# Softmax row sums in an attention block: one ones-column matmul per four key tiles, after a second vector add

## The chip, the cores and the metric

The kernel runs on all 8 cores of one Trainium2 chip. Every core executes the same program on its own data, and no core waits for another. The metric is the device time of the slowest core, in microseconds (us).

## The reference, cut to what matters

One transformer layer on x of shape (4, 2048, 2048): layer norm, latent attention with 16 heads of 128, residual, layer norm, a gated FFN with fp8 weights, residual.

```python
lat = rmsnorm(x @ wkv_a_w.T, norm_w)
kv = lat @ wkv_b_w.T
q = (x @ wq_w.T + wq_b).reshape(B, S, H, DH)        # B=4, S=2048, H=16, DH=128
scores = jnp.einsum('bqhd,bkhd->bhqk', q, k) * scale
scores = jnp.where(mask, scores, -jnp.inf)          # causal
attn = jax.nn.softmax(scores, axis=-1)
o = jnp.einsum('bhqk,bkhd->bqhd', attn, v).reshape(B, S, H * DH)
x = x + o @ out_w.T + out_b
gate = silu(layernorm(x) @ gate_w8 * gate_scale)    # 2048 -> 6144, fp8 weights
x = x + ((gate * (layernorm(x) @ up_w8 * up_scale)) @ down_w8) * down_scale
```

## The kernel before, in words

Core c takes batch entry c // 2 and one half of its 2048 positions as queries: 1024 queries, held as two blocks `qb` of 512. Keys and values are made for all 2048 positions. The stages follow each other, most of them with a barrier (every engine waits for every semaphore) between them: layer norm and transposes; the latent projection (L331); the query projection (L377); then twice (`hg` 0 and 1, eight heads each) the key projection (L440), a bound on the scores (L457 to L490), the value projection (L500) and attention (L514 to L597); then the normalization by the row sums (L602 to L627), the output projection (L665 to L699), a barrier (L700), a second layer norm (L705 to L724), gate and up (L736 to L782) and down (L789 to L857).

In attention an outer step is one head and one query block, called a block here; `pair_idx` counts the 32 blocks of a core, 16 in each half `hg`. Inside a block the loop at L545 runs over key tiles of 128, called slots: 12 slots for `qb` 0, 16 for `qb` 1. A slot is a score matmul (L551: keys as weights, 512 queries moving) into one of three PSUM banks, an exponential on ScalarE (L559) that writes a bf16 tile of 128x512 into one of eight places `PSL`, and, for the four diagonal slots of each block, a multiplication by a mask on VectorE (L566). In the blocks of `qb` 0 these are slots 0 to 3, in those of `qb` 1 slots 4 to 7. Two slots form a slot pair `p` (6 or 8 in a block). For each pair VectorE adds the two tiles (L577) into `PADD[p % 2]`, and `emit_pair(p)` queues on TensorE a ones-column matmul (L531), which adds the column sums of `PADD` to the row `PS[5]`, and then the two value matmuls (L539), which add to `PS[po]`. A program writes every engine's queue in this order: score 2p, score 2p+1, then `emit_pair(p - 1)`; after the last scores of a block `emit_pair` of its last pair comes alone. A score waits for the exponential three slots back (L550), because of its PSUM bank. The ones-column matmul waits for its `PADD` (L526), and all that stands behind it on TensorE's in-order queue waits with it: the two value matmuls and the next pair's two scores. At a block's end VectorE waits for the last value matmul, copies the row of sums (L588), which a DMA takes to its row of `F32A` (L591), and evicts the output (L594).

All waits on VectorE's work count on one semaphore, `sV`. `kb.wait` (L73) emits a wait only if that engine has not yet waited for this semaphore at that value or a higher one (L77).

In the FFN the weight loads of gate and up are issued from GpSimd (L744, L746) into two buffers; iterations 0 and 1 wait for the last matmul of the output projection, `mm_f[15]` (L741).

Of the kernel before, what the change touches and what calls it, by code (L numbers as in the profile page):

```python
# [10 lines left out]
BF16 = mybir.dt.bfloat16  # L11
# [82 lines left out]
def build_nc():  # L94
# [39 lines left out]
    sb = lambda n, sh, dt: es.enter_context(nc.sbuf_tensor(n, sh, dt))  # L134
# [42 lines left out]
    EPSC = sb("EPSC", [128, 2], F32)  # L177
    SEL = sb("SEL", [32, 384], F32)
    X4 = sb("X4", [128, 2048], BF16)

    PS = [pt(f"PS{i}", [128, 512], F32) for i in range(6)]
    PT = [pt("PT0", [128, 1024], BF16), pt("PT1", [128, 1024], BF16)]

    kb = KB(nc)
# [28 lines left out]
    try:  # L213
# [208 lines left out]
        av_ring = {}  # L422
        av_by = {}
        g_ctr = [0]
        bcast_S = [None]

        for hg in range(2):
# [86 lines left out]
            for i8 in range(8):  # L514
                h = hg * 8 + i8
                for qb in range(2):
# [2 lines left out]
                    npair = nsl // 2  # L519
                    po = 2 + (pair_idx % 2)  # L520
                    gstart = g_ctr[0]
                    rdy = {}
                    padd_by = {}

                    def emit_pair(p, i8=i8, qb=qb, po=po, gstart=gstart, npair=None, nsl=None):
                        kb.wait("tensor", "sV", padd_by[p])  # L526
                        if p == 0 and pair_idx > 0:
                            kb.wait("tensor", "sV", linv_by_pair[pair_idx - 1])
                            if pair_idx > 1:
                                kb.wait("tensor", "sV", otev_by_pair[pair_idx - 2])  # L530
                        kb.op("tensor", lambda e, p=p, isf=(p == 0), isl=(p == npair - 1): e.matmul(  # L531
                            PS[5][0:1, 0:512], ONESCb[:, 0:1], PADD[p % 2],
                            start=isf, stop=isl))
                        for i in (2 * p, 2 * p + 1):
                            kt_i = slot_lists[qb][i]
                            pi_i = (gstart + i) % 8
                            av_by[(pair_idx, i)] = av_ring[gstart + i] = kb.op(
                                "tensor", lambda e, pi_i=pi_i, kt_i=kt_i, i8=i8,
                                isf=(i == 0), isl=(i == nsl - 1), po=po: e.matmul(  # L539
                                    PS[po][:, :],  # L540
                                    BIG0[:, VOFF + kt_i * 1024 + i8 * 128:VOFF + kt_i * 1024 + i8 * 128 + 128],
                                    PSL[pi_i],
                                    start=isf, stop=isl), inc="sT")

                    for j, kt in enumerate(slots):  # L545
# [25 lines left out]
                        if j % 2 == 1:  # L571
                            p = j // 2
                            kb.wait("vector", *rdy[j - 1])
                            kb.wait("vector", *rdy[j])
                            if p >= 2:
                                kb.wait("vector", "sT", av_by[(pair_idx, 2 * (p - 2))])
                            padd_by[p] = kb.op("vector", lambda e, p=p, gstart=gstart: e.tensor_add(  # L577
                                PADD[p % 2], PSL[(gstart + 2 * p) % 8],
                                PSL[(gstart + 2 * p + 1) % 8]), inc="sV")
                            if p >= 1:  # L580
                                emit_pair(p - 1, npair=npair, nsl=nsl)
                    emit_pair(npair - 1, npair=npair, nsl=nsl)
                    g_ctr[0] += nsl
                    pgl = pair_idx % 16
                    kb.wait("vector", "sT", av_by[(pair_idx, nsl - 1)])
# [43 lines left out]
        mm_f = {}  # L629
# [106 lines left out]
        for io in range(48):  # L736
            bufp = io % 2
            if io >= 2:
                kb.wait("gpsimd", "sT", gu_mm[io - 2])
            else:  # L740
                kb.wait("gpsimd", "sT", mm_f[15])  # L741
            gin = A(gatew, io * 128, [[6144, 128], [128 * 6144, 16], [1, 128]])
            uin = A(upw, io * 128, [[6144, 128], [128 * 6144, 16], [1, 128]])
            g1 = kb.dma("gpsimd", lambda e, gin=gin, bufp=bufp: e.dma_start(  # L744
# [196 lines left out]
```

How the kernel before makes its waits and increments, by code:

```python
        def w(e, fn=fn, h=h, n=n):  # L67
            fn(e).then_inc(h, n)
# [4 lines left out]
    def wait(self, eng, name, v):  # L73
        if v is None or v <= 0:
            return
        key = (eng, name)
        if self.lastwait.get(key, 0) >= v:
            return
        self.lastwait[key] = v
        h = self.semh[name]
        self.ops[eng].append(lambda e, h=h, v=v: e.wait_ge(h, v))
```

## Time and profile before

| | us |
|---|---|
| three runs | 2452.5, 2599.4, 2604.5 (median 2599.4) |
| the profiled execution, its own time | 2458.6 |
| its span on the slowest core (core 1) | 2456.8 |
| spans of the eight cores | 2429.6 to 2456.8 |

The span is from the first to the last instruction of a core. The engines' busy times overlap, so they don't add up to it. PE is TensorE's matmuls, PEld its weight loads, DVE VectorE, ACT ScalarE, POOL GpSimd. In a timeline row "x2" are two instructions that follow each other, with the time from the start of the first to the end of the last, and the bracket is how long the engine had been idle and who ended it. The time of a matmul is its latency; back to back they follow each other faster than that.

### The profile page before, as it was taken

The numbers are of one execution on the slowest core, as the hardware profiler recorded it, in microseconds if no ns is written. First come the engines' busy times: TensorE is split into PE (matmuls) and PEld (weight loads), VectorE is DVE, ScalarE is ACT, GpSimd is POOL, SyncE is SP. The second block draws the span as 40 slices with busy tenths as digits, with TensorE's granted clock in tenths as the row PEclk, the third lists the DMA queues.
The fourth block names the chain that finished last, engine by engine and source line by source line (L and its number), as shares of the span: only waits on it lengthen the run. The fifth ranks groups of instructions, "written<-read, shape, count | busy, mean of one in ns | idle before, by whom it ended". The sixth has DMA issues, their size and how long they took to land.

```text
span 2456.8 us, 24409 instructions; the slowest of 8 cores (2429.6 to 2456.8 us)
## 1 busy us (share of the span) xinstructions
PE 1901.9 (77%) x8678; PEld 817.2 (33%) x8678; DVE 467.2 (19%) x1005; ACT 682.6 (28%) x961; POOL 236.8 (10%) x238
## 2 busy tenths in 40 slices
PE   1297944767664767657884699999999997999898
PEld 1243422211122211111442344444444443444443
DVE  3500034144434244422111300000000000000000
ACT  4621200576720766700112412211222121000000
POOL 0001100000000000000110011111111110111110
PEclk9998968899987999955997799999999998999999
DMA  6416712000011000020999378888787876988886
GB/s 149 155 18 60 71 13 28 0 1 1 1 13 22 1 1 1 1 26 0 152 157 162 77 36 40 38 38 40 37 42 35 42 36 40 80 74 77 75 79 65
DMA packets 455047, 121.94 MB, mean 50 GB/s; under 512 B 384977, under 2 KB 450706, under 8 KB 451858
## 3 DMA queue, kind: packets, MB, share of 16 engines
q0 software_dynamic: 382144, 60.90, 42.7%
q1 hardware_dynamic: 72786, 59.48, 8.4%
q8 instruction: 73, 1.20, 0.2%
q14 instruction: 44, 0.36, 0.1%
HBM read 239.83 MB, written 16.78 MB: 104 GB/s over the span
## 4 chain that ended last, share of the span: by engine, by line
PE 65%; DMA 11%; DVE 10%; ACT 7%; issue 6%; DVEq 0%; ACTq 0%; SPq 0%; POOL 0%; POOLq 0%
PE PS L759 13%; PE PS L764 13%; PE PS L818 13%; PE PS L539 3%; PE PS L377 3%; DMA WT<-outwT 3%; PE PS L677 3%; PE PS L440 3%; PE PS L619 3%; PE PS L500 2%; DVE SQB L577 2%; PE PS L331 2%; PE PS L531 2%; DMA WT<-wqT 2%; DMA F32A<-xb 2%
## 5 line engine op out<-in xcount | busy, mean ns | idle before, releaser
L818 PE MATMUL PS<-BIG,W 128*128 128x512 bf16 x1536 | 338.7, 380 | 17.1 <-DMA W<-downw 17.1
L759 PE MATMUL PS<-BIG,W 128*128 128x512 bf16 x1536 | 347.7, 379 | 1.4 <-DMA W<-upw 1.4
L764 PE MATMUL PS<-BIG,W 128*128 128x512 bf16 x1536 | 347.2, 379 | 0.0
L818 PEld LDWEIGHTS PS<-BIG,W 128*128 128x128 fp8e4 x1536 | 150.4, 98 | 193.4 <-issue 20.8
L759 PEld LDWEIGHTS PS<-BIG,W 128*128 128x128 fp8e4 x1536 | 150.3, 98 | 183.3 <-issue 3.1
L764 PEld LDWEIGHTS PS<-BIG,W 128*128 128x128 fp8e4 x1536 | 150.3, 98 | 181.2
L531 PE MATMUL PS<-SQB,ONESCb 128*1 128x512 bf16 x224 | 87.2, 389 | 114.5 <-DVE SQB L577 114.5
L559 ACT ACTIVATE X<-PS,BIASC,SCL 128x512 bf16<-128x512 f32 x224 | 157.0, 774 | 67.7 <-PE PS L551 67.7
L780 DVE TENSOR_TENSOR BIG<-PB 128x512 bf16<-128x512 bf16 x96 | 40.8, 425 | 625.0 <-ACT PB L776 625.0
L551 PE MATMUL PS<-BIG 128*128 128x512 bf16 x448 | 137.4, 389 | 24.6 <-ACT PB L559 12.0
L193 PE MATMUL PT<-IDB,XHB 128*128 128x128 bf16 x384 | 44.8, 310 | 125.4 <-DVE XHB L267 125.4
L773 ACT ACTIVATE PB<-PS,GSCc 128x512 bf16<-128x512 f32 x96 | 66.0, 688 | 269.8 <-PE PS L759 269.8
L677 PE MATMUL PS<-BIG,WT 128*128 128x512 bf16 x512 | 124.2, 399 | 19.8 <-DMA WT<-outwT 19.8
L776 ACT ACTIVATE PB<-PS,USCc 128x512 bf16<-128x512 f32 x96 | 66.0, 687 | 259.0 <-PE PS L764 259.0
L377 PE MATMUL PS<-BIG,WT 128*128 128x512 bf16 x512 | 114.8, 384 | 16.0 <-DMA WT<-wqT 15.8
L827 ACT ACTIVATE F32A<-PS,DSCc 128x512 f32<-128x512 f32 x32 | 22.0, 687 | 377.1 <-PE PS L818 377.1
L744 POOL DMA_DIRECT2D W<-gatew x48 | 54.8, 1143 | 620.5 <-PE PS L764 599.1
L440 PE MATMUL PS<-LATT,WT 128*128 128x512 bf16 x256 | 71.8, 444 | 52.4 <-DVE BIG L448 38.3
L619 PE MATMUL PS<-F32A,SEL 32*128 32x512 f32 x64 | 65.3, 1122 | 43.0 <-DVE SEL L613 43.0
L559 ACT ACTIVATE PB<-PS,BIASC,SCL 128x512 bf16<-128x512 f32 x112 | 81.0, 773 | 60.5 <-PE PS L551 60.5
L852 DVE TENSOR_TENSOR F32A<-PS,F32A 128x512 f32<-128x512 f32 x32 | 22.1, 692 | 378.1 <-PE PS L841 378.1
L687 ACT ACTIVATE F32A<-PS,OUTBc 128x512 f32<-128x512 f32 x32 | 22.0, 687 | 242.2 <-PE PS L677 242.2
(106 smaller groups left out, 1566.5 us busy)
## 6 DMA issues: line engine op xcount, KB each, us to landing
F32A<-xb SPq DMA_DIRECT2D x16, 1024.0 KB, 5.1
W<-gatew POOLq DMA_DIRECT2D x48, 256.0 KB, 8.6
W<-upw POOLq DMA_DIRECT2D x48, 256.0 KB, 10.4
W<-downw POOLq DMA_DIRECT2D x48, 256.0 KB, 9.2
WT<-wqT POOLq DMA_DIRECT2D x16, 512.0 KB, 6.7
F32A<-xb SPq DMA_DIRECT2D x32, 256.0 KB, 5.0
WT<-outwT POOLq DMA_DIRECT2D x16, 512.0 KB, 9.2
res_scr<-F32A SPq DMA_DIRECT2D x32, 256.0 KB, 5.5
```

The lines of the kernel that those rows point to most:

```text
L377: mmct = kb.op("tensor", lambda e, c=c, pi=pi, ot=ot, qb=qb: e.matmul(PS[pi][:, :], WT[:, (ot % 2) * 2048 + c * 128:(ot % 2) * 2048 + (c + ...
L440: mmct = kb.op("tensor", lambda e, c=c, tb=tb, i8=i8: e.matmul(PS[tb][:, :], WT[:, (i8 % 2) * 2048 + c * 128:(i8 % 2) * 2048 + (c + 1) * 128],
L531: kb.op("tensor", lambda e, p=p, isf=(p == 0), isl=(p == npair - 1): e.matmul(PS[5][0:1, 0:512], ONESCb[:, 0:1], PADD[p % 2], start=isf, s ...
L539: isf=(i == 0), isl=(i == nsl - 1), po=po: e.matmul(PS[po][:, :], BIG0[:, VOFF + kt_i * 1024 + i8 * 128:VOFF + kt_i * 1024 + i8 * 128 + 12 ...
L551: t_s = kb.op("tensor", lambda e, sb_=sb_, i8=i8, kt=kt, qb=qb, h=h: e.matmul(sb_[:, :], BIG0[:, KOFF + i8 * 2048 + kt * 128:KOFF + i8 * 2 ...
L559: exp_ring[g] = kb.op("scalar", lambda e, pi=pi, sb_=sb_, qb=qb, kt=kt: e.activation(PSL[pi], sb_[:, :], AFT.Exp, bias=BIASC[:, qb * 16 + ...
L619: mm_by[p] = mmb = kb.op("tensor", lambda e, s=s: e.matmul(PS[2 + s][:, 0:512], SEL[0:32, s * 128:(s + 1) * 128], F32A[0:32, 2560:3072], s ...
L677: mmct = kb.op("tensor", lambda e, c=c, pi=pi, dt=dt, qb=qb: e.matmul(PS[pi][:, :], WT[:, (dt % 2) * 2048 + c * 128:(dt % 2) * 2048 + (c + ...
L759: mmg = kb.op("tensor", lambda e, c=c, qb=qb, bufp=bufp, pb=pb: e.matmul(PS[pb][:, :], W8[:, bufp * 2048 + c * 128:bufp * 2048 + (c + 1) * ...
L764: mmu = kb.op("tensor", lambda e, c=c, qb=qb, bufp=bufp, pb=pb: e.matmul(PS[pb + 1][:, :], W8[:, 4096 + bufp * 2048 + c * 128:4096 + bufp ...
L773: s_g = kb.op("scalar", lambda e, io=io, pb=pb: e.activation(PB[:, 0:512], PS[pb][:, :], AFT.Silu, scale=GSCc[:, io:io + 1]), inc="sS")
L818: isl=(t3 == 2 and cc == 15): e.matmul(PS[pi][:, :], W8[:, slot * 2048 + cc * 128:slot * 2048 + (cc + 1) * 128], fuse_ap(c, qb), start=isf ...
```

## The change

Two edits.

1. In attention the results of two adds are added once more: after each odd pair, VectorE adds `PADD[0]` and `PADD[1]` into a new tile `PADD2`, and one ones-column matmul on `PADD2` takes the place of the two on `PADD`. The old `emit_pair` is split: `emit_lmm(q2)` queues the ones-column matmul for the pairs 2*q2 and 2*q2+1, and `emit_av(p)` the two value matmuls. For even `p` from 2 on, `emit_lmm` of the two pairs before comes right ahead of `emit_av(p - 1)`; at a block's end `emit_lmm` of the last two pairs comes ahead of the last `emit_av`. A new write to `PADD` waits for the last `PADD2` add instead of for a value matmul. `PADD2` is one tile: its next write waits for the ones-column matmul that read it.
2. In the FFN the wait of GpSimd for `mm_f[15]` ahead of the first two weight loads is taken out.

```diff
+    PADD2 = sb("PADD2", [128, 512], BF16)
...
-                    def emit_pair(p, i8=i8, qb=qb, po=po, gstart=gstart, npair=None, nsl=None):
+                    def emit_lmm(q2, nq=nq):
+                        kb.wait("tensor", "sV", padd2_by[q2])
+                        if q2 == 0 and pair_idx > 0:
+                            kb.wait("tensor", "sV", linv_by_pair[pair_idx - 1])
+                        lmm_by[q2] = last_lmm[0] = kb.op(
+                            "tensor", lambda e, isf=(q2 == 0), isl=(q2 == nq - 1): e.matmul(
+                                PS[5][0:1, 0:512], ONESCb[:, 0:1], PADD2[:, 0:512],
+                                start=isf, stop=isl), inc="sT")
+
+                    def emit_av(p, i8=i8, qb=qb, po=po, gstart=gstart, nsl=None):
                         kb.wait("tensor", "sV", padd_by[p])
-                        if p == 0 and pair_idx > 0:
-                            kb.wait("tensor", "sV", linv_by_pair[pair_idx - 1])
-                            if pair_idx > 1:
-                                kb.wait("tensor", "sV", otev_by_pair[pair_idx - 2])
-                        kb.op("tensor", lambda e, p=p, isf=(p == 0), isl=(p == npair - 1): e.matmul(
-                            PS[5][0:1, 0:512], ONESCb[:, 0:1], PADD[p % 2],
-                            start=isf, stop=isl))
+                        if p == 0 and pair_idx > 1:
+                            kb.wait("tensor", "sV", otev_by_pair[pair_idx - 2])
...
                             if p >= 2:
-                                kb.wait("vector", "sT", av_by[(pair_idx, 2 * (p - 2))])
+                                kb.wait("vector", "sV", padd2_by[p // 2 - 1])
+                            elif last_padd2[0]:
+                                kb.wait("vector", "sV", last_padd2[0])
...
+                            if p % 2 == 1:
+                                q2 = p // 2
+                                kb.wait("vector", "sV", padd_by[p])
+                                if q2 >= 1:
+                                    kb.wait("vector", "sT", lmm_by[q2 - 1])
+                                elif last_lmm[0]:
+                                    kb.wait("vector", "sT", last_lmm[0])
+                                padd2_by[q2] = last_padd2[0] = kb.op("vector", lambda e: e.tensor_add(
+                                    PADD2[:, 0:512], PADD[0], PADD[1]), inc="sV")
                             if p >= 1:
-                                emit_pair(p - 1, npair=npair, nsl=nsl)
-                    emit_pair(npair - 1, npair=npair, nsl=nsl)
+                                if p % 2 == 0 and p >= 2:
+                                    emit_lmm((p - 2) // 2)
+                                emit_av(p - 1, nsl=nsl)
+                    emit_lmm((npair - 2) // 2)
+                    emit_av(npair - 1, nsl=nsl)
...
             if io >= 2:
                 kb.wait("gpsimd", "sT", gu_mm[io - 2])
-            else:
-                kb.wait("gpsimd", "sT", mm_f[15])
```

## Rows read from the trace of the kernel before

**Rows 1.** The windows view: both attention halves, the key projection, gate/up. First its columns.

```profile
core 1: us, PE busy (x) PEld busy (x) DVE busy (x) ACT busy (x) POOL busy (x), PEclk, DMA share, GB/s
475.00:695.00 220.00, 153.88 (x554) 43.14 (x554) 91.25 (x205) 155.11 (x223) 7.30 (x15) 0.98 0.00 1
...
702.00:760.00 58.00, 35.98 (x128) 13.65 (x128) 19.47 (x32) 0.00 (x0) 4.46 (x6) 0.86 0.17 16
...
820.00:1048.00 228.00, 159.72 (x555) 43.95 (x555) 91.28 (x205) 159.02 (x226) 7.30 (x15) 0.96 0.00 1
...
1386.00:2054.00 668.00, 664.18 (x3076) 300.61 (x3073) 41.77 (x98) 133.30 (x193) 105.01 (x92) 1.00 0.77 37
```

**Rows 2.** The groups of instructions by line over the whole execution.

```profile
L531 PE MATMUL PS<-SQB,ONESCb 128*1 128x512 bf16 x224 | 87.2, 389 | 114.5 <-DVE SQB L577 114.5
...
L577 DVE TENSOR_TENSOR SQB<-X 128x512 bf16<-128x512 bf16 x112 | 47.6, 425 | 102.2 <-PE PS L551 49.0 <-PE PS L539 29.8 <-ACT X L559 20.4
```

**Rows 3.** The waits of the first attention half, 475 to 695 us.

```profile
PE PS L531 <- DVE SQB L577: 57.3, 73, 1.4
...
ACT X L559 <- PE PS L551: 33.1, 30, 2.0
...
ACT PB L559 <- PE PS L551: 29.7, 27, 2.0
```

**Rows 4.** The timeline inside a block of `qb` 0 (weight loads left out).

```profile
480.10 1.45 ACT L559 ACTIVATE X<-PS,BIASC,SCL 128x512 bf16<-128x512 f32 x2 [0.27 <-PE PS L551]
...
481.72 0.42 DVE L577 TENSOR_TENSOR SQB<-X 128x512 bf16<-128x512 bf16 x1 [1.29 <-PE PS L551]
...
482.29 0.38 PE L531 MATMUL PS<-SQB,ONESCb 128*1 128x512 bf16 x1 [0.37 <-DVE SQB L577]
...
482.60 0.60 PE L539 MATMUL PS<-X,BIG 128*128 128x512 bf16 x2
...
483.04 0.59 PE L551 MATMUL PS<-BIG 128*128 128x512 bf16 x2
...
483.52 1.45 ACT L559 ACTIVATE SQB<-PS,BIASC,SCL 128x512 bf16<-128x512 f32 x2 [0.27 <-PE PS L551]
...
485.14 0.42 DVE L577 TENSOR_TENSOR SQB<-SQB 128x512 bf16<-128x512 bf16 x1 [1.29 <-ACT SQB L559]
```

**Rows 5.** The timeline over a block's end, and the ends of the two blocks behind it.

```profile
486.46 0.81 PE L551 MATMUL PS<-BIG 128*128 128x512 bf16 x3
486.73 0.68 DVE L588 COPY LINV<-PS 1x512 f32<-1x512 f32 x1 [1.17 <-PE PS L539]
486.94 2.79 ACT L559 ACTIVATE X<-PS,BIASC,SCL 128x512 bf16<-128x512 f32 x4 [1.97 <-PE PS L551]
...
502.27 0.68 DVE L588 COPY LINV<-PS 1x512 f32<-1x512 f32 x1 [1.24 <-PE PS L539]
...
514.32 0.68 DVE L588 COPY LINV<-PS 1x512 f32<-1x512 f32 x1 [1.24 <-PE PS L539]
```

**Rows 6.** The timeline: a vector add behind a vector mask that it needs, twice.

```profile
475.21 0.42 DVE L566 TENSOR_TENSOR PB<-PB,MASKS 128x512 bf16<-128x512 bf16 x1 [0.24 <-ACT PB L559]
475.74 0.43 DVE L577 TENSOR_TENSOR SQB<-PB 128x512 bf16<-128x512 bf16 x1
...
491.84 0.43 DVE L566 TENSOR_TENSOR PB<-PB,MASKS 128x512 bf16<-128x512 bf16 x1 [0.24 <-ACT PB L559]
492.44 0.43 DVE L577 TENSOR_TENSOR SQB<-PB 128x512 bf16<-128x512 bf16 x1 [0.17 <-DVE PB L566]
```

**Rows 7.** The same loop at low granted clock: the windows view, then the timeline.

```profile
561.40:564.70 3.30, 3.30 (x9) 0.73 (x9) 0.42 (x1) 2.47 (x4) 0.00 (x0) 0.52 0.00 0
...
561.53 0.59 PE L531 MATMUL PS<-SQB,ONESCb 128*1 128x512 bf16 x1
562.05 1.03 PE L539 MATMUL PS<-X,BIG 128*128 128x512 bf16 x2
562.87 1.06 PE L551 MATMUL PS<-BIG 128*128 128x512 bf16 x2
563.61 1.45 ACT L559 ACTIVATE SQB<-PS,BIASC,SCL 128x512 bf16<-128x512 f32 x2 [0.83 <-PE PS L551]
```

**Rows 8.** The groups of instructions by line: the first weight loads of gate and up.

```profile
L759 PE MATMUL PS<-BIG,W 128*128 128x512 bf16 x1536 | 347.7, 379 | 1.4 <-DMA W<-upw 1.4
```

More of the change, by code:

```diff
@@ L424, in build_nc @@
         g_ctr = [0]
+        last_lmm = [None]
+        last_padd2 = [None]
         bcast_S = [None]
@@ L521, in build_nc @@
                     gstart = g_ctr[0]
+                    nq = npair // 2
                     rdy = {}
                     padd_by = {}
-                    def emit_pair(p, i8=i8, qb=qb, po=po, gstart=gstart, npair=None, nsl=None):
-                        kb.wait("tensor", "sV", padd_by[p])
-                        if p == 0 and pair_idx > 0:
-                            kb.wait("tensor", "sV", linv_by_pair[pair_idx - 1])
-                            if pair_idx > 1:
-                                kb.wait("tensor", "sV", otev_by_pair[pair_idx - 2])
-                        kb.op("tensor", lambda e, p=p, isf=(p == 0), isl=(p == npair - 1): e.matmul(
-                            PS[5][0:1, 0:512], ONESCb[:, 0:1], PADD[p % 2],
-                            start=isf, stop=isl))
+                    padd2_by = {}
+                    lmm_by = {}
+                    def emit_lmm(q2, nq=nq):
[7 more added lines that the diff above has]
+                    def emit_av(p, i8=i8, qb=qb, po=po, gstart=gstart, nsl=None):
+                        kb.wait("tensor", "sV", padd_by[p])
+                        if p == 0 and pair_idx > 1:
+                            kb.wait("tensor", "sV", otev_by_pair[pair_idx - 2])
                         for i in (2 * p, 2 * p + 1):
```

## The prediction

> **What bounds the kernel now.** I read the windows view first, cut at the stages, because a change to attention is worth what that stage lets through. In gate and up TensorE is busy for 664 of 668 us. In the two attention halves it is busy for 154 of 220 and 160 of 228 us, and ScalarE, the next engine, for 155 and 159; nothing is full there [rows 1]. So the stage is a chain of engines waiting for each other. The groups and the waits name its links: TensorE stands for 114.5 us ahead of the ones-column matmul L531, always for the vector add L577 [rows 2], and ScalarE stands for 33.1 and 29.7 us in the first half for scores [rows 3].
>
> The timeline gives the chain link by link [rows 4]. From start to start: vector add 481.72, ones-column matmul 482.29 (+0.57, of which 0.42 is the add), value matmuls 482.60 (+0.31), scores 483.04 (+0.44), exponentials 483.52 (+0.48), the next add on this chain 485.14 (+1.62: two exponentials, 1.45, and 0.17). Sum 3.42 us. That add belongs to the slot pair two further on. Two such chains interleave, one of even and one of odd pairs, so two pairs take 3.42 us: the exponentials that start at 480.10 and at 483.52 are those of one chain, 3.42 apart. ScalarE has 2 x 1.45 = 2.90 of work in it at most and isn't the bound.
>
> Check at the length of a block. From the first score at a block's start: 0.48 to the exponentials, 2.79 for four of them, 0.17 to the add of the odd pair (3.44), then the odd chain turns 2 times (6 pairs) or 3 times (8 pairs), then add to scores 0.57 + 0.31 + 0.44 = 1.32. That makes 11.60 and 15.02 us. Measured between ends of blocks: 514.32 - 502.27 = 12.05 and 502.27 - 486.73 = 15.54 [rows 5]. The rest, about 0.5 in each, I put down to the masks. The odd chain thus sets the length of a block, and the block's last pair is an odd one.
>
> **The change, part by part.**
>
> *Ones-column matmuls removed.* 224 become 112 [rows 2]. Each holds the queue for 0.31 us (start of L531 to start of L539, [rows 4]). But which leave the chain? Even pairs lose theirs: their chain becomes 3.42 - 0.31 = 3.11 us. Odd pairs keep one, since `emit_lmm` stands ahead of `emit_av` of the odd pair, also at the block's end. Had the removed ones been on the path they would be worth 112 x 0.31 = 34.7 us. By the block sum above they lie on the even chain, which has to wait for the odd one in TensorE's order, so I count nothing. What hides them is the odd chain; without that cover they are worth the 34.7.
>
> *Vector adds inserted.* 3 for each of 16 blocks and 4 for each of 16: 112. Each stands behind the odd pair's add and waits for its result; the ones-column matmul waits for it, and behind that on TensorE the odd pair's value matmuls and the next two scores, and so the next exponentials. Its duration isn't in the trace; the nearest rows are L577, same shape and type, 0.425 us [rows 2]. The wait of a vector instruction for the one before it: mask end 475.63 to add 475.74 is 0.11, mask end 492.27 to add 492.44 is 0.17 [rows 6]. So an insertion costs 0.53 to 0.60 us, and the odd chain becomes 3.95 to 4.02 us. All 112 stand on it: 59 to 67 us. I take the middle, 63.
>
> The Trainium skill has another price: VectorE: DVE Perf Modes, section on the TRN2 errata, gives (58 + elements / speed-up) cycles at 0.96 GHz for SBUF to SBUF. With 512 elements at 2x that is an estimate of 0.33 us where this trace has 0.425. By it the adds would cost 0.10 us less each, 11 us in all. The measured row decides.
>
> *Other new waits.* The write to `PADD` now waits for the last `PADD2` add on VectorE's own queue; that lies a pair back. `PADD2` waits for the ones-column matmul that read it, two pairs back. Both are over before the exponentials are in: nothing, and if the second wasn't, it would come to a part of one 0.38 us matmul. The old wait for a value matmul two pairs back goes; in the steady rows the add starts 0.17 us after the exponentials' end in any case [rows 4], so it gives nothing. VectorE itself has room: 91 of 220 us plus 56 x 0.425 = 24.
>
> *The clock.* In the halves the granted clock is 0.98 and 0.96 [rows 1], that is 2.4 GHz with short stretches at 1.2. A stretch at half clock lowers the mean by half its share, so 2 x 0.02 x 220 + 2 x 0.04 x 228 = 27 us are low. In one, TensorE had stood for the masks after a block's end, and then the links were 0.52, 0.82 and 0.74 instead of 0.31, 0.44 and 0.48 [rows 7]: 0.85 us more for a turn of the chain. Now TensorE has 554 matmuls in the first half's 220 us (2.5 per us); after the change it has 56 fewer in some 31 us more (2.0 per us). The stage nearest to that is the key projection, 128 matmuls of this width in 58 us (2.2 per us), and its granted clock is 0.86: 28% of the time low [rows 1]. The same share of 448 + 63 us is 143 us, 116 more than now. A low turn takes 4.0 + 0.85, so each low us costs 0.85 / 4.85 = 0.175 us: 20 us. Bounds: 0 if the pauses stay as they are, and 90 if every turn is low (112 x 0.85 = 95, less the 27 x 0.175 = 5 already paid). I take 20, from the nearest row.
>
> *The FFN wait.* The barrier at L700 has made GpSimd wait for TensorE's semaphore at a value that `mm_f[15]` is part of, and `kb.wait` drops a wait already covered. So no instruction goes: 0 us. If one did, the only stall on these loads is 1.4 us [rows 8].
>
> **Sum.** 2458.6 (the profiled execution's own time; its span is 1.8 less) + 63 + 20 = 2541.6, say 2542 us, +3.4%. This stands on the level of the lowest of the three runs (2452.5); the median, 2599.4, lies 5.7% above that execution, and no trace here shows such a run.
>
> **The rivals.**
>
> 1. *The add is hidden and the matmul pays* (opposite side). If VectorE were done before TensorE gets to the ones-column matmul, 34.7 us would go: 2424. For it speaks only that VectorE is 41% busy. Against it: TensorE waits there for the add 73 times in the first half, 57.3 us, 0.78 each [rows 3]. It decides once the sum add ends before TensorE reaches the matmul, some 0.8 + 0.5 us earlier than these rows make it. Chance 0.04.
>
> 2. *The chains share.* If even and odd chains evened out through ScalarE's and TensorE's order, each two pairs would cost the mean of the two changes: (0.56 - 0.31) / 2 = 0.125 us, 112 of them 14 us: 2473, within 2%. For it: both go through the same queues. Against it: the even chain cannot start its scores before the odd one's value matmuls, and the block's end is the odd one. Chance 0.10, with what lies between it and the forecast.
>
> 3. *The clock falls for good.* 67 + 90 us: 2616. The mechanism is a longer pause of TensorE in every turn (the 0.53 to 0.60 of the add) with fewer matmuls between. Against it: at the low clock the same loop kept TensorE busy through the whole stretch [rows 7], and the clock then came back. The Trainium skill speaks for it: TensorE: Matmul & The Clock Gate, section HAM oscillation, says that pauses between bursts send the array back to half rate each time anew. Chance 0.07, again with what lies above my range.
>
> 4. *The FFN edit starts the loads sooner*: at most 1.4 us, changes no chance.
>
> **How the numbers follow.** The forecast has 0.79. Its own range runs from 59 + 0 less a margin for the sharing (2510) to 67 + about twice the clock's price (2566). Rivals 1 and 2 hold 0.14 and rival 3 0.07; none of the three can be left out whole without the others passing 2 in 10, so the range is the forecast's, a few us wider at both ends for what lies between the cases: 2505 to 2572 should hold 0.8. This kernel's measurement can tell about 2%, 49 us, from no change. Below -2% there is nearly nothing, since even all of 34.7 isn't 49: 0.02. Within: the rest of rivals 1 and 2, 0.12 (a cheaper add alone, 0.42 with no wait behind it, would still be 47 us). Slower: the forecast and rival 3, 0.86.
>
> **What would show it.** In the changed kernel's timeline inside a block: an add of `PADD2` 0.53 to 0.60 us behind the odd pair's add; the ones-column matmul 0.57 behind that; odd adds 3.95 to 4.02 apart, where now it is 3.42; value matmuls of even pairs 0.57 behind their add. Ends of blocks 12.05 + 1.7 and 15.54 + 2.2 us apart. In the windows view attention halves some 40 us longer, with a granted clock near 0.86; the FFN unchanged. I am wrong if the add to `PADD2` ends before TensorE has finished the work queued ahead of its matmul, if it takes much less than 0.42 us, or if the clock stays as it is (then 2522) or stays low (then 2616).

## The result and the profile after

| | before | after |
|---|---|---|
| median of the runs, us | 2458.0 (10 runs) | 2537.7 (9 runs) |
| ratio to before, 95% interval | | 1.0325, 1.0302 to 1.0348 |
| span of the profiled execution, slowest core | 2456.8 | 2533.1 |
| first to last sum copy of each attention half, both added up | 423.1 | 502.1 |

The change makes the kernel 3.25% slower, some 80 us, and attention holds all of it. (Single executions of any of these kernels are some per cent longer, with one die at a lower clock; the ratios leave them out, and two of the three times shown ahead of the prediction were such.)

The last row of the table is read from the copies of the sums that end the blocks, 15 blocks in each half. The page of the changed kernel, engine row:

```profile
PE 1901.2 (75%) x8410; PEld 822.8 (32%) x8566; DVE 517.3 (20%) x1117; ACT 687.0 (27%) x961; POOL 237.2 (9%) x238
```

PEld 8566 is 112 less than before and DVE 1117 is 112 more: the matmuls that went, the adds that came. (The count of PE itself lacks some records in this trace; before, loads and matmuls were 8678 each.) POOL is x238 in both kernels. The wait that the FFN edit takes out isn't counted there, but `kb.wait` never emitted it, since the barrier at L700 had covered its value: the edit changes nothing in the program.

The windows view of the changed kernel: both attention halves, then the 668 us of gate and up. It answers to [rows 1] and has its columns: stretch, length, busy time of PE, PEld, DVE, ACT and POOL with the number of instructions, granted clock, DMA share, GB/s.

```profile
475.00:736.00 261.00, 160.62 (x489) 46.34 (x498) 114.65 (x258) 156.60 (x220) 7.34 (x15) 0.85 0.00 1
861.00:1129.00 268.00, 163.15 (x494) 46.91 (x504) 116.55 (x262) 161.23 (x227) 7.34 (x15) 0.84 0.00 1
1449.00:2117.00 668.00, 654.14 (x3002) 300.11 (x3064) 49.16 (x111) 138.86 (x199) 105.14 (x92) 0.99 0.78 38
```

The halves, 220 and 228 us before, are 261 and 268 long; ScalarE does nearly the same work in them, 157 and 161 us (155 and 159 before); the granted clock went from 0.98 and 0.96 to 0.85 and 0.84. Gate and up is as it was: 665.4 us from its first to its last matmul, 665.5 before (its PE count lacks records too).

The groups by line answer to [rows 2]:

```profile
L536 PE MATMUL PS<-PADD,ONESCb 128*1 128x512 bf16 x112 | 48.7, 435 | 148.2 <-DVE PADD L599 148.2
...
L599 DVE TENSOR_TENSOR PADD<-SQB 128x512 bf16<-128x512 bf16 x112 | 47.6, 425 | 17.2 <-DVE SQB L589 13.1 <-PE PS L561 0.7
```

Half as many ones-column matmuls (L536), but TensorE stands longer ahead of them: 148.2 us, 1.32 for each, where 224 had 114.5. All of it ends with the new add, L599. It takes 425 ns, as the first add does.

One turn of the odd chain in the timeline of the changed kernel, at full clock; it answers to [rows 4], and one row from the next turn is added:

```profile
513.62 0.43 DVE L589 TENSOR_TENSOR SQB<-SQB 128x512 bf16<-128x512 bf16 x1 [2.38 <-ACT SQB L569]
...
514.22 0.42 DVE L599 TENSOR_TENSOR PADD<-SQB 128x512 bf16<-128x512 bf16 x1 [0.17 <-DVE SQB L589]
514.78 0.38 PE L536 MATMUL PS<-PADD,ONESCb 128*1 128x512 bf16 x1 [0.79 <-DVE PADD L599]
515.09 0.61 PE L549 MATMUL PS<-SQB,BIG 128*128 128x512 bf16 x2
...
515.54 0.59 PE L561 MATMUL PS<-BIG 128*128 128x512 bf16 x2
...
516.01 1.45 ACT L569 ACTIVATE X<-PS,BIASC,SCL 128x512 bf16<-128x512 f32 x2 [0.79 <-PE PS L561]
517.56 0.43 DVE L589 TENSOR_TENSOR SQB<-X 128x512 bf16<-128x512 bf16 x1 [1.75 <-ACT X L569]
...
518.74 0.38 PE L536 MATMUL PS<-PADD,ONESCb 128*1 128x512 bf16 x1 [2.17 <-DVE PADD L599]
```

From start to start: first add to second +0.60, to the ones-column matmul +0.56, value matmuls +0.31, scores +0.45, exponentials +0.47, next add +1.55. Sum 3.94, where it was 3.42. The second add costs 0.60; the last link is 0.07 shorter than before (1.55 for 1.62). In the next turn TensorE stands for 2.17 us ahead of the ones-column matmul.

The ends of four blocks on core 1 of the changed kernel answer to [rows 5]:

```profile
552.90 0.68 DVE L612 COPY LINV<-PS 1x512 f32<-1x512 f32 x1 [1.24 <-PE PS L549]
570.50 0.68 DVE L612 COPY LINV<-PS 1x512 f32<-1x512 f32 x1 [1.24 <-PE PS L549]
...
637.35 0.68 DVE L612 COPY LINV<-PS 1x512 f32<-1x512 f32 x1 [1.24 <-PE PS L549]
651.00 0.68 DVE L612 COPY LINV<-PS 1x512 f32<-1x512 f32 x1 [1.24 <-PE PS L549]
```

A long block takes 17.60 and a short one 13.65. These are, to 0.01 us, the shortest of their kinds, and nearly all others are longer by a stretch at the low clock. Before, the shortest were 12.05 and 15.47, and most blocks took just that (the 15.54 of [rows 5] is the first whole block of a half).

The two can now be told apart. 30 blocks (16 long and 14 short) at their shortest are 416.2 us before and 472.4 after: 56.2 us, or 0.53 for each second add. Measured as a mean of the eight cores they are 422.3 and 501.9. What lies over the shortest, 6.1 and 29.5 us, is 23.4 more. Nearly all of it lies in blocks that hold a stretch at the low clock (all but 1.0 us before and 0.1 after), so I put it down to the clock.

### The profile page after: what moved, and what is told of

Read it like the earlier page. It is cut to its first block, busy times and chain, and to the rows that moved or that the text cites. A ratio compares the mean times of both kernels' runs of the same rounds, so it can differ in the third digit from the quotient of the medians.

```text
span 2533.1 us, 24253 instructions; the slowest of 8 cores (2504.6 to 2533.1 us)
## 1 busy us (share of the span) xinstructions
PE 1901.2 (75%) x8410; PEld 822.8 (32%) x8566; DVE 517.3 (20%) x1117; ACT 687.0 (27%) x961; POOL 237.2 (9%) x238
## 4 chain that ended last, share of the span: by engine, by line
PE 63%; DVE 11%; DMA 11%; ACT 7%; issue 7%; DVEq 1%; ACTq 0%; SPq 0%; POOL 0%; POOLq 0%
PE PS L781 13%; PE PS L786 13%; PE PS L840 13%; PE PS L549 4%; PE PS L378 3%; PE PS L701 3%; DMA WT<-outwT 3%; PE PS L443 3%; PE PS L643 3%; PE PS L503 2%; PE PS L332 2%; ACT X L569 2%; PE PS L561 2%; DMA WT<-wqT 2%; DVE SQB L589 2%
## 5 line engine op out<-in xcount | busy, mean ns | idle before, releaser
L561 PE MATMUL PS<-BIG 128*128 128x512 bf16 x440 | 165.8, 458 | 23.4 <-ACT PB L569 10.5
L536 PE MATMUL PS<-PADD,ONESCb 128*1 128x512 bf16 x112 | 48.7, 435 | 148.2 <-DVE PADD L599 148.2
L549 PE MATMUL PS<-X,BIG 128*128 128x512 bf16 x220 | 83.6, 468 | 19.8 <-DVE SQB L589 18.9
## 6 DMA issues: line engine op xcount, KB each, us to landing
W<-downw POOLq DMA_DIRECT2D x48, 256.0 KB, 10.1
```

The lines of the kernel that those rows point to most:

```text
L549: isf=(i == 0), isl=(i == nsl - 1), po=po: e.matmul(PS[po][:, :], BIG0[:, VOFF + kt_i * 1024 + i8 * 128:VOFF + kt_i * 1024 + i8 * 128 + 12 ...
L561: t_s = kb.op("tensor", lambda e, sb_=sb_, i8=i8, kt=kt, qb=qb, h=h: e.matmul(sb_[:, :], BIG0[:, KOFF + i8 * 2048 + kt * 128:KOFF + i8 * 2 ...
```

## The experiments

The ratios are against the kernel before on the same chip. The other two columns are read from one profiled execution of each kernel: "shortest block" is what one takes at full clock, between two copies of the sums; "30 blocks" is the mean of the cores from the first to the last such copy of each half.

| kernel | ratio (95%) | shortest short, long block | 30 blocks |
|---|---|---|---|
| before | 1 | 12.05, 15.47 | 422.3 |
| changed | 1.0325 (1.0302 to 1.0348) | 13.64, 17.59 | 501.9 |
| half_ones | 1.0002 (0.9976 to 1.0029) | 12.05, 15.46 | 424.2 |
| add_only | 1.0286 (1.0261 to 1.0311) | 13.63, 17.58 | 491.8 |
| values_first | 1.0044 (1.0019 to 1.0069) | 12.34, 15.85 | 437.2 |
| double_add | 1.0698 (1.0635 to 1.0760) | none undisturbed | 583.7 |
| waits_first | 0.9986 (0.9963 to 1.0008) | 11.91, 15.26 | 413.5 |
| early | 0.9756 (0.9699 to 0.9813) | 10.71, 13.46 | 369.0 |
| after_early | 1.0091 (1.0063 to 1.0119) | 12.34, 15.85 | 441.3 |
| after_early2 | 0.9718 (0.9681 to 0.9755) | 10.42, 13.09 | 357.6 |
| early_deferred | 0.9730 (0.9675 to 0.9785) | 10.41, 13.15 | 360.6 |
| carry | 0.9645 (0.9600 to 0.9691) | 9.22, 12.02 (usual 12.64) | 331.2 |
| carry_first | 0.9572 (0.9526 to 0.9618) | 9.08, 11.82 (usual 12.37) | 324.8 |
| carry_deferred | 0.9492 (0.9457 to 0.9527) | 8.67, 10.75 (usual 11.65) | 306.7 |

In the last three kernels the shortest long block is the last one of each half, which no other block follows; all the other long blocks take about the usual figure, with no low clock anywhere in the 30 blocks. Of early only two executions stand behind the ratio, and its interval doesn't settle whether the whole kernel gains as much as 2%.

### half_ones: the matmuls gone, the second add too

This kernel leaves half of the key tiles out of the row sums. The edit, against the changed kernel:

```diff
-                                PS[5][0:1, 0:512], ONESCb[:, 0:1], PADD2[:, 0:512],
+                                PS[5][0:1, 0:512], ONESCb[:, 0:1], PADD[1],
...
-                                PADD[p % 2], PSL[(gstart + 2 * p) % 8],
+                                PADD[p % 2], PSL[(gstart + 2 * p - 2 * (p % 2)) % 8],
...
-                                padd2_by[q2] = last_padd2[0] = kb.op("vector", lambda e: e.tensor_add(
-                                    PADD2[:, 0:512], PADD[0], PADD[1]), inc="sV")
+                                padd2_by[p // 2] = last_padd2[0] = padd_by[p]
```

> The changed kernel without its second vector add: the odd pair's ones-column matmul reads the odd pair's own sum tile and waits for that alone; even pairs have no ones-column matmul. The row sums then hold two of every four key tiles (the odd pair's add takes the first tile of the even pair and the last of its own), so the normalization is wrong. Theory (the even pairs' matmuls lie off the chain): undisturbed blocks stay at 12.05 and 15.47 us, as before; only the clock may fall a little with 9 matmuls instead of 10 in 3.42 us: 2455 to 2470 us. Rival (they are on the path, and the change only lost because of the add): 35 us less than before, 2423 us.

Three block ends in its timeline:

```profile
497.11 0.68 DVE L603 COPY LINV<-PS 1x512 f32<-1x512 f32 x1 [1.24 <-PE PS L549]
509.15 0.68 DVE L603 COPY LINV<-PS 1x512 f32<-1x512 f32 x1 [1.24 <-PE PS L549]
524.62 0.68 DVE L603 COPY LINV<-PS 1x512 f32<-1x512 f32 x1 [1.24 <-PE PS L549]
```

12.04 and 15.47, the lengths of the kernel before, and a ratio of 1.000. So the 112 even ones-column matmuls that the change removes were off the chain: worth nothing, and not the 35 us that their own time would make. That takes away the gain in rival 1, measured by itself, and the share of it in rival 2: had the two chains shared, the blocks would have been shorter.

### add_only: the second add, all matmuls kept

```diff
-                        kb.wait("tensor", "sV", padd_by[p])
+                        kb.wait("tensor", "sV", padd2_by[p // 2] if p % 2 else padd_by[p])
...
+                            if p % 2 == 1:
+                                kb.wait("vector", "sV", padd_by[p])
+                                padd2_by[p // 2] = last_padd2[0] = kb.op("vector", lambda e: e.tensor_add(
+                                    PADD2[:, 0:512], PADD[0], PADD[1]), inc="sV")
```

> The kernel before with all its ones-column matmuls, plus the second vector add, for which the odd pair's ones-column matmul waits (nothing reads its result). Theory (each add stands on the odd chain): undisturbed blocks at 12.05 + 3 x 0.53 = 13.64 and 15.47 + 4 x 0.53 = 17.59 us, as in the changed kernel, 59 us in all; what it then differs from the changed kernel is the clock alone: with 10 matmuls instead of 9 in a turn the granted clock should lie between 0.97 and 0.84, the total at 2520 to 2530 us. Rival (the clock falls because of the longer pause, whatever the number of matmuls): as the changed kernel, 2538 us, clock 0.84.

Its windows over the two attention halves, and three block ends:

```profile
475.00:739.00 264.00, 170.55 (x560) 45.55 (x560) 116.74 (x263) 161.63 (x227) 7.32 (x15) 0.91 0.00 1
861.00:1126.00 265.00, 170.32 (x560) 45.55 (x560) 117.47 (x264) 161.48 (x227) 7.33 (x15) 0.91 0.00 1
```

```profile
544.41 0.68 DVE L596 COPY LINV<-PS 1x512 f32<-1x512 f32 x1 [1.23 <-PE PS L542]
558.05 0.68 DVE L596 COPY LINV<-PS 1x512 f32<-1x512 f32 x1 [1.24 <-PE PS L542]
575.63 0.68 DVE L596 COPY LINV<-PS 1x512 f32<-1x512 f32 x1 [1.24 <-PE PS L542]
```

13.64 and 17.58: the changed kernel's blocks to 0.01 us. The second add alone gives the whole longer chain. The same length is made up differently, though: here the second add has a single wait ahead of it and costs 0.53, and the old wait for the value matmul still stands; in the changed kernel it costs 0.60 inside a block, and 0.07 comes back where that wait went.

```profile
542.22 0.43 DVE L581 TENSOR_TENSOR SQB<-X 128x512 bf16<-128x512 bf16 x1 [2.53 <-ACT X L562]
542.75 0.42 DVE L586 TENSOR_TENSOR PADD<-SQB 128x512 bf16<-128x512 bf16 x1
...
556.96 0.38 PE L534 MATMUL PS<-SQB,ONESCb 128*1 128x512 bf16 x1 [1.75 <-DVE PADD L586]
```

Its median was 2522.2, as the theory put it, and the granted clock 0.91 lies between 0.97 and 0.84. Over the shortest blocks it has 491.8 - 472.4 = 19.4 us, where before has 6.1 and the changed kernel 29.5. So of the clock's 23.4 us, 13.3 come with the second add and 10.1 when the even pairs' matmuls then go. The removal of work cost time here. Two limits: taken in the other order the split is another (half_ones, without the second add, is 424.2 against 422.3, 1.9 us), so the two act together; and a removed matmul also lengthens TensorE's longest usual pause, from 1.75 to 2.17 us, so these runs don't show whether the clock fell for the number of matmuls or for the pause.

### values_first: who waits behind the second add

```diff
-                                if p % 2 == 0 and p >= 2:
-                                    emit_lmm((p - 2) // 2)
                                 emit_av(p - 1, nsl=nsl)
-                    emit_lmm((npair - 2) // 2)
+                                if p % 2 == 0 and p >= 2:
+                                    emit_lmm((p - 2) // 2)
                     emit_av(npair - 1, nsl=nsl)
+                    emit_lmm((npair - 2) // 2)
```

> The changed kernel with the two value matmuls queued ahead of the ones-column matmul. Theory (the cost is that the value matmuls and scores wait behind the second add): the value matmuls start 0.57 us behind the odd pair's add, the ones-column matmul 1.17 behind it, the scores 0.31 later, where now it is 1.92: a turn of 3.94 - 0.44 = 3.50 us, 9 us in all over before, and a clock between 0.97 and 0.84: 2465 to 2480 us. Rival (VectorE's extra work or the lost matmul itself costs): above 2510 us.

Its timeline over a turn:

```profile
511.08 0.42 DVE L589 TENSOR_TENSOR SQB<-SQB 128x512 bf16<-128x512 bf16 x1 [1.26 <-ACT SQB L569]
511.65 0.59 PE L549 MATMUL PS<-SQB,BIG 128*128 128x512 bf16 x2 [0.67 <-DVE SQB L589]
511.68 0.43 DVE L599 TENSOR_TENSOR PADD<-SQB 128x512 bf16<-128x512 bf16 x1 [0.17 <-DVE SQB L589]
512.25 0.38 PE L536 MATMUL PS<-PADD,ONESCb 128*1 128x512 bf16 x1
...
512.56 0.60 PE L561 MATMUL PS<-BIG 128*128 128x512 bf16 x2
...
514.59 0.43 DVE L589 TENSOR_TENSOR SQB<-X 128x512 bf16<-128x512 bf16 x1 [1.68 <-ACT X L569]
```

The value matmuls run beside the second add, 0.57 behind the first; the ones-column matmul comes at 1.17, the scores at 1.48. The turn is 3.51 us (forecast 3.50). The same adds and the same number of matmuls as in the changed kernel, and 69 of its 80 us are gone (ratio 1.0044). The cost was not the add but its place ahead of work that doesn't need it.

### double_add: one more instruction behind the add

```diff
+                                mid = kb.op("vector", lambda e: e.tensor_add(
+                                    PADD2[:, 0:512], PADD[0], PADD[1]), inc="sV")
+                                kb.wait("vector", "sV", mid)
+                                padd2_by[q2] = last_padd2[0] = kb.op("vector", lambda e: e.tensor_max(
+                                    PADD3[:, 0:512], PADD2[:, 0:512], PADD2[:, 0:512]), inc="sV")
```

> The changed kernel with one more vector instruction of the same shape (a maximum of PADD2 with itself into another tile, so the values stay) between the second add and the ones-column matmul. Theory (whatever VectorE does behind the odd pair's add stands whole on the odd chain): 0.42 + 0.10 more in every turn, undisturbed blocks at 13.64 + 3 x 0.53 = 15.23 and 17.59 + 4 x 0.53 = 19.71 us, 59 us more than the changed kernel before the clock; with TensorE in longer pauses the clock gives another 5 to 25: 2600 to 2625 us. Rival (the adds run beside other work and something else set the changed kernel's time): within 15 us of 2538.

The time, 2612.9, is in the range; but the kernel before took some 2444 us on this chip and not 2458, so by the ratio the loss is 171 us where the forecast allows 142 to 167. The blocks can't be compared as I meant to: none was free of the low clock (the shortest were 15.93 and 20.31). The turn can, in a stretch of its timeline at full clock, and the windows show the clock:

```profile
517.56 0.43 DVE L590 TENSOR_TENSOR SQB<-SQB 128x512 bf16<-128x512 bf16 x1 [3.07 <-ACT SQB L570]
518.16 0.42 DVE L600 TENSOR_TENSOR PADD<-SQB 128x512 bf16<-128x512 bf16 x1 [0.17 <-DVE SQB L590]
518.69 0.42 DVE L603 TENSOR_TENSOR PADD<-PADD 128x512 bf16<-128x512 bf16 x1
...
522.04 0.42 DVE L590 TENSOR_TENSOR SQB<-X 128x512 bf16<-128x512 bf16 x1 [2.40 <-ACT X L570]
```

```profile
486.00:781.00 295.00, 185.50 (x478) 50.04 (x476) 133.51 (x302) 151.21 (x212) 7.31 (x15) 0.71 0.00 1
```

The turn is 4.48 us, 0.54 over 3.94, and the clock was lower again, 0.71. Each of the two instructions behind the odd pair's add stands whole on the chain.

### waits_first: where the missing 0.07 us went

```diff
+                            if p >= 2:
+                                kb.wait("vector", "sT", av_by[(pair_idx, 2 * (p - 2))])
                             kb.wait("vector", *rdy[j - 1])
                             kb.wait("vector", *rdy[j])
-                            if p >= 2:
-                                kb.wait("vector", "sT", av_by[(pair_idx, 2 * (p - 2))])
```

> The kernel before with one wait of VectorE moved: the wait for the value matmul two pairs back, which is over long before, stands ahead of the two waits for the exponentials and no longer behind them. In the changed kernel an add with two waits starts 0.10 us behind the exponentials and one with a third wait behind them 0.17. Theory (each wait that stands behind the late one costs 0.07 us): the odd chain turns in 3.35 instead of 3.42 us, in 2 turns of a short and 3 of a long block, and the block's last add is a turn's too: undisturbed blocks at 11.91 and 15.26, 5 to 8 us in all, 2450 us. Rival (the third wait was late by its own event, the value matmul): nothing changes, 12.05 and 15.47.

The shortest blocks are 11.91 and 15.26: 0.14 and 0.21 less, 2 and 3 times 0.07, as forecast. Two rows of its timeline show the link:

```profile
508.04 1.45 ACT L559 ACTIVATE SQB<-PS,BIASC,SCL 128x512 bf16<-128x512 f32 x2
...
509.60 0.43 DVE L577 TENSOR_TENSOR SQB<-SQB 128x512 bf16<-128x512 bf16 x1 [0.92 <-PE PS L539]
```

The exponentials end at 509.49 and the add starts 0.11 later, where in [rows 4] it is 0.17. In 30 blocks it saves 8.8 us; in the whole time the ratio's interval (0.9963 to 1.0008) doesn't tell it from nothing. The changed kernel had this gain too: the wait for the value matmul behind the odd pair's exponentials was gone.

### early: the chain cut instead

```diff
+                        if j % 2 == 0 and j >= 4:
+                            emit_pair(j // 2 - 2, npair=npair, nsl=nsl)
...
-                            if p >= 1:
-                                emit_pair(p - 1, npair=npair, nsl=nsl)
+                    emit_pair(npair - 2, npair=npair, nsl=nsl)
                     emit_pair(npair - 1, npair=npair, nsl=nsl)
```

> The kernel before with one thing moved: slot pair p-1 is added up and multiplied behind score 2p+2 instead of ahead of it, so the next pair's first score no longer waits for the vector add. Theory (the loop is a chain from exponential to add to matmuls to score): only the second score of the pair stays behind the add; it comes 0.17 + 0.42 + 0.15 + 0.31 + 0.44 + 0.48 = 1.97 us after the exponential, where ScalarE needs 3 x 0.67 = 2.01 for the three exponentials between. ScalarE becomes the bound, 1.34 us a pair instead of 1.71: blocks of about 10.1 and 12.8 us plus the masks, clock near 1, 2385 us. Rival (TensorE's own work bounds attention, so only fewer matmuls would help): no change, 2458 us.

The profiled span was 2386.1, the ratio 0.976. One score moved ahead of the matmuls that wait for VectorE takes 53 us out of 422 with every instruction kept. This is the proof from the other side: attention was a chain, and TensorE's amount of work did not bound it. The blocks, 10.71 and 13.46, are still longer than the 10.1 and 12.8 of the theory; masks, which it left open, and block ends weren't told apart here.

### after_early, after_early2 and early_deferred: does the halving pay once the wait is hidden

after_early queues the changed kernel's value matmuls as early does, and its ones-column matmul behind score 4q+5:

```diff
+                        if j % 2 == 0 and j >= 4:
+                            emit_av(j // 2 - 2, nsl=nsl)
+                        if j % 4 == 1 and j >= 5:
+                            emit_lmm(j // 4 - 1)
```

> The changed kernel with its value matmuls queued behind the next pair's first score, as in the run early, and its ones-column matmul one score later still. Theory (once ScalarE bounds the loop, neither the second add nor half of the ones-column matmuls count, but at a block's end the scores wait for the second add): as early inside a block, 0.16 us more at each of 32 ends: 2385 to 2400 us, not faster than early (2388). Rival (halving the ones-column matmuls pays when its wait is hidden): 10 us or more under early.

A miss: 2468 us. The timeline says why:

```profile
503.73 0.42 DVE L593 TENSOR_TENSOR SQB<-X 128x512 bf16<-128x512 bf16 x1 [1.96 <-ACT X L573]
504.32 0.43 DVE L603 TENSOR_TENSOR PADD<-SQB 128x512 bf16<-128x512 bf16 x1 [0.17 <-DVE SQB L593]
504.90 0.38 PE L536 MATMUL PS<-PADD,ONESCb 128*1 128x512 bf16 x1 [1.31 <-DVE PADD L603]
...
505.20 0.39 PE L561 MATMUL PS<-BIG 128*128 128x512 bf16 x1
505.43 0.59 PE L549 MATMUL PS<-X,BIG 128*128 128x512 bf16 x2
```

The ones-column matmul stood ahead of the next score and of the odd pair's value matmuls, and TensorE waited there for the second add, 1.31 us. I had placed it one pair too soon. after_early2 puts it behind score 4q+7:

```diff
-                        if j % 4 == 1 and j >= 5:
+                        if j % 4 == 3 and j >= 7:
```

> As the run after_early, but the ones-column matmul of four tiles stands behind score 4q+7 and no longer behind score 4q+5, so that the odd pair's value matmuls and the scores around them are queued ahead of it; in after_early it stood ahead of them and waited there for the second add. Theory: the loop is then free of the second add and bounded by ScalarE; blocks of 10.71 + 0.16 and 13.46 + 0.16 us (the end of a block still waits for the second add), 5 us over early: 2385 to 2400. Rival (the halved ones-column matmuls pay once they are hidden): blocks under 10.71 and 13.46, 2380 or less. Second rival (VectorE's second adds themselves are in the way of its masks and adds): blocks near 11.5 and 14.5, 2415.

Now 2378 us, with shortest blocks of 10.42 and 13.09, less than early's and not more: the theory's direction was wrong, and this looked like the rival, a gain from halving. But the ones-column matmul also stood elsewhere than in early. The control keeps all of them and moves each behind the next score:

```diff
+                        if j % 2 == 0 and j >= 4:
+                            emit_av(j // 2 - 2, nsl=nsl)
+                        if j % 2 == 1 and j >= 5:
+                            emit_ones(j // 2 - 2)
```

> The control for after_early2, whose undisturbed blocks took 10.42 and 13.09 us where early took 10.71 and 13.46: the run early with its full number of ones-column matmuls, each moved behind the next score as in after_early2, and no second add. If after_early2 gained by where the ones-column matmul stands, this gains at least as much: blocks of 10.42 and 13.09 or up to 0.1 less, since the end of a block waits for no second add; 2370 to 2378 us. If it gained because there are half as many, this stays near 10.71 and 13.46, 2388 us.

10.41 and 13.15 with all matmuls and no second add; 30 blocks take 360.6 us, after_early2 357.6. The long block is 0.06 over after_early2's and the time, 2381.9, over the forecast 2370 to 2378, but 8 of the 11 us by which after_early2 beats early in 30 blocks came from the place of the matmul. At most 3 us are left for halving and second add together, and the two ratios (0.9718 and 0.9730) don't differ.

### carry, carry_first and carry_deferred: what beats both kernels

carry is early with the order kept up over a block's end: the last two pairs are multiplied behind the next block's scores 0 and 2.

```diff
+                        if j % 2 == 0 and len(waiting) > 1:
+                            f, q = waiting.pop(0)
+                            f(q)
...
+                            waiting.append((emit_pair, p))
```

> The run early with the order carried over the block ends: the last two slot pairs of a block are added up and multiplied behind the first scores of the next block, and the copies of the sums and of the output follow there. Theory (what early leaves, 10.71 and 13.46 us against 8.0 and 10.7 us of exponentials, is ScalarE standing at block ends for TensorE's last matmuls): blocks of 8.1 and 10.8 us, 2.6 less for each of 32, 2305 to 2330 us. Rival (VectorE's two copies of 0.68 and 0.67 us now stand ahead of a sum add and take their place): blocks of 9 and 12 us, 2350 us.

30 blocks take 331.2 us. A short block is 9.22, the rival's figure and not the theory's 8.1. A usual long one is 12.64, over both (12 and 10.8), and so is the time, 2362.6. Its timeline at a block's start shows VectorE's copy in the way:

```profile
527.70 0.68 DVE L552 COPY LINV<-PS 1x512 f32<-1x512 f32 x1 [0.25 <-PE PS L542]
...
528.53 0.38 PE L534 MATMUL PS<-SQB,ONESCb 128*1 128x512 bf16 x1 [0.57 <-DVE LINV L552]
```

The new block's first ones-column matmul waits 0.57 us for the copy that frees its PSUM row, and scores stand behind it.

carry_first moves the wait as waits_first does:

```diff
+                            if last_av[p % 2]:
+                                kb.wait("vector", "sT", av_by[last_av[p % 2]])
                             kb.wait("vector", *rdy[j - 1])
                             kb.wait("vector", *rdy[j])
-                            if last_av[p % 2]:
-                                kb.wait("vector", "sT", av_by[last_av[p % 2]])
```

> The run carry with VectorE's wait for the value matmul ahead of its waits for the exponentials. Theory (0.07 us for a wait that stands behind the late one): two pairs inside a block take 2.74 us in carry and ScalarE's four exponentials 2.68, so at most 0.06 us for each two pairs and at the ends of blocks a little more: blocks of 9.0 to 9.2 and 11.8 to 12.0 us, 0 to 8 us in all, 2345 to 2355. Rival: nothing changes (the adds are off the chain).

324.8 us: 6.4 less, at the upper end of the forecast; the usual long block, 12.37, is over the forecast blocks. carry_deferred then moves each ones-column matmul behind the next score, so that nothing else stands behind the copy:

```diff
+                        elif j % 2 == 1 and ones_due:
+                            f, q = ones_due.pop(0)
+                            f(q)
```

> The fastest so far, carry_first (blocks of 9.08 and 11.82 us), with each ones-column matmul moved behind the next score. ScalarE's exponentials alone are 8.0 and 10.7 us. Theory: the 0.31 us of the ones-column matmul leaves the way of each pair's second score, most of it at the masks and at the block starts: blocks of 8.6 to 9.0 and 11.3 to 11.7, 2330 to 2340 us. Rival (VectorE's copies at a block's start are what is left): unchanged, 2340 to 2345.

306.7 us, 2327 in all, a little more gained than forecast. Its windows over some twelve blocks of the first half:

```profile
486.00:613.00 127.00, 117.31 (x437) 35.87 (x436) 71.62 (x166) 120.79 (x176) 6.34 (x13) 1.00 0.01 1
```

ScalarE is busy for 95% and TensorE for 92% with the clock at 1.00: here attention comes close to the bound of an engine, and which of the two it is was not tested. It is 5.1% faster than the kernel before (interval 4.7 to 5.4%), with every ones-column matmul still in it.

## Why the prediction missed, and what in it held

What failed is the level that the sum stands on. The prediction adds 83 us to 2458.6, the profiled execution, and gives 2542 as the time; it names the shown median of 2599.4 only to say that no trace shows such a run, and never settles which of the two is the time that the forecast is to be read against. Beside that median 2542 is a gain of 57 us, or 2.2%, while the argument, the chances and the +3.4% say a loss. The runs showed 2458.0 as the median of ten for the kernel before and 2537.7 after: a loss of 79.7 us. So the base of the sum turned out right, by a choice whose only stated reason was that a trace existed for it, and the median beside which its number stood was not the kernel's level.

The mechanism held, and the range of 2505 to 2572 holds the 2537.7. In attention the kernel lost 79.6 us in 30 blocks, where the sum was 83 for 32. Two terms of that sum were mis-sized in opposite directions, so that part of the closeness is luck. In 30 blocks they come to 5.3 us too much and some 3 to 4 us too little:

- **The old wait for a value matmul that goes.** This term was put at nothing, because the add starts 0.17 us behind the exponentials in any case. A wait that is over but stands behind the late one is a part of that 0.17: without it 0.10 to 0.11 is left. That is 0.07 for a turn, 76 turns in 30 blocks (3 in a long one, 2 in a short one), 5.3 us; waits_first shows it alone. It also explains both figures of [rows 6]: the add with 0.17 has such a wait behind its late one, the other has none.
- **The clock.** Forecast a granted 0.86 and 20 us, by the key projection's clock [rows 1]; measured 0.85 and 0.84, and 23.4 in 30 blocks. The low time, by the records of the clock, went from 14 to 157 us within the 30 blocks of a core: 143 more, where the prediction had 116, and 0.164 us for each low us, where it had 0.175. The nearest row gave the right size, but nothing here shows why it should. What the prediction did not split is that 10 of the 23.4 come only when the matmuls go as well: it named both the pause and the count, and add_only takes the matmuls back.

The other terms:

- **The even pairs' matmuls are worth nothing.** Held: half_ones, ratio 1.0002. With it rivals 1 and 2 fall.
- **Each second add stands on the odd chain, 0.53 to 0.60 us, 63 in all.** The place held in all four tests (add_only, values_first, double_add, the timeline), and the size too: the first of a block costs 0.53 and the others 0.60, since there a second wait, long over, stands behind the late one. That is 61.5 us in 30 blocks (30 and 76 of them), some 65 in 32. Less the 5.3 of the old wait it is the 56.2 measured: 0.53 net for each.
- **The check at a block's length** left 0.5 us for the masks. No run tests that; the sum doesn't use it.
- **Rival 3**, a clock that stays low, did not occur: it fell in many short stretches and came back. The Trainium skill's section HAM oscillation (TensorE: Matmul & The Clock Gate) describes that coming and going between bursts; there the pauses are waits for DMA, while here they are the chain's own, 2.17 us in the row at 518.74, and it shows as a mean of 0.85, in double_add as 0.71.
- **The price by the page.** By the Trainium skill (VectorE: DVE Perf Modes, section on the TRN2 errata) the add was estimated at 0.33 us; the new group measured 0.425, as the old one did. The same section says that this formula comes out too low for a single copy, with a fixed term of some 150 cycles measured; with that term the estimate is 0.42.
- **The FFN edit** is worth nothing: the wait was never emitted.

## What to carry to other kernels

Where no engine is full, count the turns of the chain between engines, and not the work of the busiest one: in this loop an instruction cost its time only if something on the chain was queued behind it, and then it cost it whole. In an in-order queue one wait holds up all that stands behind it: put what waits last (here a sum that nobody needs soon) behind the work that others need; in attention the same instructions then took 306.7 us for 422.3. Fewer matmuls in a loop that is bound elsewhere can cost time twice, as here, by what replaces them and by the clock. And say against which time a forecast is to be read before giving it in us.

## What I had not expected of the hardware

- A wait of VectorE that has long been met costs 0.07 us if it stands behind the one that is met last: 0.17 against 0.10 to 0.11 us from the release to the start, in the changed kernel, in waits_first and, where two waits stand ahead of the second add, in the rows of values_first.
- Taking 112 of 1120 matmuls out of attention, with blocks of the same undisturbed length, moved the granted clock from 0.91 to 0.85 and 0.84 and cost 10 us in 30 blocks (add_only against the changed kernel, one profiled execution of each: 489.0 to 494.7 us over the cores of one, 499.2 to 504.5 over those of the other; the intervals of the whole kernels' ratios overlap a little). In half_ones, with shorter pauses, the same removal moved 30 blocks only from 422.3 to 424.2.
